# The last two layers of a four-layer convolution kernel: the quantised convolution, its update and its square move one step nearer to the scaling of their tile

## The reference, cut to what matters

```python
def _L2_conv_ref(x, weight_int8, scale_weight, bias):      # 3x3, zero padding
    scale_input = jnp.max(jnp.abs(x_cl)) / 2.0 ** (ACTBIT - 1)
    x_q = jnp.round(jnp.clip(x_cl / scale_input, -n, n))    # n = 127
    acc = lax.conv_general_dilated(x_q, w_hwio, ...)
    out = acc * (scale_input * scale_weight) + bias
def _L3_conv_ref(x, weight):                               # circular 3x3 by FFT
    ...
x = x + _L2_conv_ref(_gn(x), L2_conv_weight_int8, L2_conv_scale_weight, L2_conv_bias)
x = x + _L3_conv_ref(_gn(x), L3_conv_weight)
return x
```

## Time and profile before

| | before |
|---|---|
| median of 3 runs (lowest, highest) | 6229.66 us (6224.24, 6241.02) |
| profiled execution: its own time | 6232.09 us |
| profiled execution: span of the core | 6230.2 us |
| granted TensorE clock, mean | 0.949 |
| PE matmul busy | 5335.2 us, 86% |
| DVE busy | 5053.6 us, 81% |
| ACT busy | 4538.9 us, 73% |
| DMA moved | 958.88 MB, 154 GB/s |

### The profile page before, as it was taken

The page is one execution under the profiler, slowest core; times in us unless marked ns, Lnnn a source line. Parts: engine busy times, 40 slices in busy tenths (PEclk is TensorE's granted clock), DMA queues, the critical chain, the costliest instruction groups (busy, mean ns, idle before and its releaser), DMA issues. The chain is left out here.

```text
span 6230.2 us, 202732 instructions
## 1 busy us (share of the span) xinstructions
PE 5335.2 (86%) x63882; PEld 3402.6 (55%) x63882; DVE 5053.6 (81%) x10660; ACT 4538.9 (73%) x8793; POOL 3153.6 (51%) x5676
## 2 busy tenths in 40 slices
PE   0379979979979979979989989968898988989889
PEld 0058748748748748747757757833343433434334
DVE  5879979979979989988998998986676766767664
ACT  2578768868868867867876666768787877878775
POOL 3178768758858858858857858921111110111102
PEclk9889989989989989999999999989999999999999
DMA  6516616616616625625624524646676766767665
GB/s 203 158 47 209 204 40 206 207 46 201 206 53 190 208 69 171 208 88 159 206 95 115 159 84 113 177 94 155 166 204 163 204 162 159 200 162 196 168 163 139
DMA packets 535621, 958.88 MB, mean 154 GB/s; under 512 B 121946, under 2 KB 126938, under 8 KB 532826
## 3 DMA queue, kind: packets, MB, share of 16 engines
q1 hardware_dynamic: 467546, 798.95, 45.0%
q10 hardware_dynamic: 67456, 151.01, 7.8%
HBM read 560.40 MB, written 287.60 MB: 136 GB/s over the span
## 5 line engine op out<-in xcount | busy, mean ns | idle before, releaser
L1655 PE MATMUL pC<-xs,taps 128*128 128x512 f16 x4608 | 1095.8, 383 | 106.7 <-DMA xhalo<-xs 100.4
L981 PE MATMUL pM<-gw,xh 64*128 64x256 f16 (+1 forms) x24960 | 1130.7, 244 | 5.5 <-DVE yt L1141 4.7
L981 PEld LDWEIGHTS pM<-gw,xh 64*128 64x128 f16 x24960 | 972.5, 95 | 133.4 <-issue 12.0
L1551 POOL TENSOR_TENSOR xn<-xn,one_col 128x1 f32<-128x1 f32 x520 | 170.4, 328 | 1406.4 <-ACT xn L1585 1406.4
L1655 PEld LDWEIGHTS pC<-xs,taps 128*128 128x128 f16 x4608 | 449.3, 98 | 672.1 <-DVE xs L1705 90.2
L1571 ACT ACTIVATE scaled<-X,qbias,qscale 128x512 f32 (+1 forms) x512 | 413.3, 808 | 327.8 <-DMA X<-after_layer 297.0
L742 POOL TENSOR_TENSOR X<-X,zo 128x256 f32 (+1 forms) x512 | 372.5, 727 | 548.3 <-DVE zo L1105 548.3
L279 PE MATMUL pM<-X,mix0s 64*64 64x512 f32 x2304 | 530.1, 634 | 134.5 <-DVE X L1073 108.5
L723 POOL TENSOR_TENSOR X<-X,rl 128x512 f32 x384 | 478.4, 1275 | 270.8 <-ACT rl L772 270.7
L1593 ACT ACTIVATE xs<-xn 128x1028 f16<-128x1028 f32 x520 | 546.8, 1051 | 86.7 <-POOL xn L1552 86.2
L1712 DVE SCALAR_TENSOR_TENSOR result<-pC,X 128x512 f32<-128x512 f32 x512 | 352.4, 688 | 303.3 <-DMA out_dram<-result 181.4
(11 more groups left out here) (249 smaller groups left out, 13574.2 us busy)
## 6 DMA issues: line engine op xcount, KB each, us to landing
gw<-row_weights SPq DMA_DIRECT2D x520, 288.0 KB, 3.4
after_layer<-X SPq DMA_DIRECT2D x512, 256.0 KB
out_dram<-result SPq DMA_DIRECT2D x512, 256.0 KB
X<-in_x_dram SPq DMA_DIRECT2D x448, 256.0 KB
X<-after_layer ACTq DMA_DIRECT2D x224, 512.0 KB, 5.7
stage<-in_x_dram SPq DMA_DIRECT2D x192, 512.0 KB
xhalo<-xs SPq DMA_DIRECT2D x504, 96.4 KB, 3.7
qhalo<-q SPq DMA_DIRECT2D x496, 96.2 KB, 3.9
```

What stands on the lines that cost most here:

```text
L981: nc.tensor.matmul(pY[:, r, col:col + nd * P], row(xh, r)[:, k, p, ri, off:off + P], weights(r, q_, d, nd, ri), start=ri == 0 and off == 1 ...
L1655: nc.tensor.matmul(bank, taps3[:, d, wh], xs[:, h, own, d:d + W], start=d == 0 and n == 0, stop=False)
```

## The change

conv2 takes tile t - 16 instead of t - 17 in turn t, update tile t - 17 instead of t - 18, and square3 tile t - 18 instead of t - 19. The ring and bank numbers follow. Nothing else is moved; there is one turn less in each stretch.

```diff
-                TURNS = DELAY + J + 7 
+                TURNS = DELAY + J + 6
...
-                            if c2 and live(u, 7, J + 7):
-                                square3(b + 1, u - 7, k)
+                            if c2 and live(u, 6, J + 6):
+                                square3(b + 1, u - 6, k)
...
                     def conv2(b, w, k, g):
-                        slot = (k - 1) % RING
+                        slot = k
                         m = slot // 2
                         fixed = 16 if m == 0 or isinstance(w, int) and w >= J - 2 else 0
-                        done = w // RING if isinstance(w, int) else g - 3 + (k + 7) // 8
+                        done = w // RING if isinstance(w, int) else g - 2
...
-                            nc.tensor.matmul(pC2[:, slot % 4], taps2[:, d], q[:, k, d:d + W], start=d == 0, stop=False)
+                            nc.tensor.matmul(pC2[:, slot % 4], taps2[:, d], q[:, (k + 1) % RING, d:d + W], start=d == 0, stop=False)
...
-                            w, v = t - DELAY - 5, t - 6
+                            w, v = t - DELAY - 4, t - 6
...
-                        nc.vector.scalar_tensor_tensor(out=Xf[:, w], in0=pC2[:, (k - 2) % 4], scalar=oscale2[:, :], in1=Xf[:, w],
+                        nc.vector.scalar_tensor_tensor(out=Xf[:, w], in0=pC2[:, (k - 1) % 4], scalar=oscale2[:, :], in1=Xf[:, w],
...
-                            if c2 and live(u, 6, J + 6):
-                                update(b + 1, u - 6, k)
+                            if c2 and live(u, 5, J + 5):
+                                update(b + 1, u - 5, k)
```

## The result

The changed kernel takes 6272.94 us (median of 6 runs, 6266.14 to 6281.5), the kernel before 6238.45 us beside it (6224.24 to 6242.6). The ratio is 1.006, 95% interval 1.0046 to 1.0074: slower, by 34 us between the medians and by 29 to 46 us by the interval. The forecast was 6299 us, +69 on 6229.66; the direction and the range held, the size is twice what came.

What follows compares the result with a forecast made beforehand. It took PE to bound the joint stretches, other engines close behind, and the halo copy to bind after the change. 6232.1 + 17 + 47 + 5 = 6301, less 2.4 for the median: 6299 us, range 6245 to 6360.

Steps and rivals of the forecast that it cites:

- First stretch: Image 0 alone: the loop from copy to copy takes 3.56 us a pair instead of 3.00; +17 us.
- One turn more in each joint stretch: Joint stretches: 55 turns instead of 54, +3.47 us an image, partly covered in the drain; +5 us.
- The pair in the joint stretch: Joint stretches: the halo copy to conv2 becomes the bound, 7.40 us a pair instead of 7.15; +47 us.
- The slack of before: Joint stretches of the kernel before: conv2 had three turns, 10.4 us, for its copy, some 3 us to spare.
- ACT's load loop as the pace of before: Joint stretches: ACT's loop through the load, 7.08 us a pair, sets much of the 7.15.
- (a): Rival: the joint stretch hides it, ACT's load loop is the true pace; +17 + 5, 6252 us; chance 0.26.
- (b): Rival: nothing softens in the joint stretches, landings stay at 4.2 us; +17 + 95 + 10, 6352 us; chance 0.18.
- (c): Rival: a tile less in every drain, seven save 14 us, faster at 6216 us; chance 0.04.
- (d): Rival: the change doesn't bite, conv2 is bound by another wait than the copy; 6230 us; chance 0.06.
- The forecast's own signs: First-stretch copies 3.56 us apart, PE idle for the copy, joint stretches 200 to 207 us, shorter landings, fewer store waits.

Runs made afterwards that it cites:

- three against three: Traces of three kernels with PE in the new order in the seven periods against three in the old one: 19 us more in the mean.
- first_only: Kernel before with the change in the first stretch (image 0) alone, order of before elsewhere: 1.0029 (1.0018 to 1.004), +18 us.
- conv3_first: Kernel before with the change in the seven joint periods alone and conv3 in front of conv2 in PE's turn: 1.0002 (0.9991 to 1.0013).
- one turn nearer: Kernel before with conv2 one turn behind quant of tile w + 2 in the seven joint periods: 1.1156 (1.1134 to 1.1178), +720 us.

## Why the prediction was right, and where it wasn't

- **First stretch: right mechanism, +17 forecast, 21 to 24 in the traces, 18 (11 to 25) in the runs.** The loop of two pairs was 7.12 us on paper and is 2 x 3.66 = 7.32 at full clock, mostly because update starts 0.18 us after conv2's last matmul, where I allowed 0.04. The clock, which I left out, adds 0.06 to 0.14 a pair.
- **One turn more in each joint stretch, covered in part in the drain: right, +5 forecast.** Joint turns went from 54 to 55, 7 x 3.47 = 24.3 us. The drains, to the last conv2, fell by 141.1 - 122.2 = 18.9 in these two profiles, which leaves 5.4, and by 12 in three against three, which leaves 12; the bounds were 0 and 24. The last load now goes out 1.1 us after the last finish in the mean, where it was 2.8: the slack was used up.
- **The pair in the joint stretch: the step that was mis-sized, +47 forecast.** I put it at 7.40, between 7.25 and 7.65. It is 7.17. The loop was right in kind: 2.88 to the issue, 3.84 of landing, 0.43 until conv2 starts (means over the joint stretches), 7.15 together. The landing came at the lower of my two values for the middle (3.8 and 4.2): with PE behind it fell from 4.3 to 3.84, and the issue came 0.30 sooner than in the earlier trace rows. What I put on top for slower landings and for scatter between two loops did not come. Against other executions with PE in the old order (7.10 in first_only, 7.13 in conv3_first) the pair rose by 0.04 to 0.07, 8 to 13 us, not 47.
- **Where these 8 to 13 us lie: not in the pair at all.** From tile 6 to tile 52 the pair is 7.13 against 7.14. They are the first pairs of each stretch, at the lower clock. The forecast had no term for the clock.
- **The slack of before: misread.** I gave the copy some 3 us to spare in the kernel before, from rows of the seventh stretch. There it had 3.5 in the mean; over the seven stretches it had 1.15 in the mean and 0.75 in the median. In the other stretches DVE, held by the stores, ran behind PE, and the copy went out 5.4 us after its turn's conv2 in the mean over all seven, not 3.18. The change takes a turn of distance, and most of this lag goes with it: 2.88. That is why a distance shorter by 3.47 us costs the pair next to nothing.
- **ACT's load loop as the pace of before: half right.** Loads matter (-82 us with half of them), but the stores were a limit too, which I had named only as a wait of DVE. I had read the 175 us as lag and not as a pace.
- **Rivals.** (a), the joint stretch hides it, gave +22 and lay nearer than the forecast: +34 stands between it and +69. It was right that the pair barely grows, though not because ACT's loads paced everything. That the total still came out inside the range is in part the range's width: it was made to hold (a) too. (b) is out: landings fell. (c) is out: the drains got shorter by 2.7 us each, but only because conv3 was late by a turn. (d) is out: conv2 now follows the landing by 0.29 us in the median, and one turn nearer costs 720 us.
- **The forecast's own signs.** The copies of the first stretch moved apart, PE waits for the copy, its landing is shorter and DVE's wait for stores smaller, as said. But joint stretches are 195 to 201 us and not 200 to 207, the pair stayed near 7.15, and the drains got shorter by more than 2 us each. The last two had been named as signs that the forecast is wrong; they came, and its largest term, +47, did not.

## What to carry to other kernels

In a pipeline written in turns, price a shorter distance by the loop that it closes: add up start to issue, issue to landing and landing to start from rows, and compare with the turns that are left. Where two limits are near each other, taking slack from one costs only what it exceeds the other by, and the name of a wait doesn't tell which of them paces: move one of them by a turn both ways to see. Read the slack from all stretches and not from the smoothest one. Look at the start of a stretch by itself: a longer wait of PE there can also cost the clock behind it. A latency under load is no constant: what is won by issuing earlier can come back as a later landing.

## What was not expected

- The wait for the first copy costs twice: 3.4 to 4.8 us without work for PE, and behind it, for a while, a granted clock of 1.2 GHz, with which the first pair takes 8.6 us instead of 6.9 (seventh stretch), about 8 us over seven stretches.
- A copy of 96 KB between partitions lands in 2.7 us in the first stretch, 3.1 with half of the loads left out, 3.8 in the changed kernel and 4.2 in the kernel before (medians); issued 0.39 us earlier, it took 0.34 longer.
- With half of each load left out the kernel gained 82 us, twice the 41 us by which PE was short of its own pace in the joint stretches of before (1351.9 - 7 x 187.3); the drains gave 33, the fronts 12.
- Executions of the same code differ by up to 18 us in the seven periods (1816.7 and 1798.7), as much as the effect that was looked for.
